# One core, four layers: lag of two tiles in the bit stage, bf16 openings of three recurrent stages, unread products at an RNN's end

## The reference

```python
# _L0_cond2_ref and _L3_cond2_ref: an LSTM over 256 steps for 8 rows of 128
a = xw_t + prev_h @ Wh
i, f, o = sigmoid of three quarters of a;  g = tanh(the last quarter)
next_c = f * prev_c + i * g;  next_h = o * tanh(next_c)
# layer 2: the same LSTM (_L2_cond_ref); then a gated delta rule over its output
S = tanh(beta * S + (v - S @ kn) x kn);  out = Sq * silu(Sq), Sq = S @ q
# then a plain RNN over x + y @ W_out:  h = tanh(h @ Wh + xW_t)
# then _L2_ffn_ref, the bit feed-forward (128 -> 512 -> 128, 2048 tokens)
wq = clip(round(w * scale), -1, 1) / scale
xq = clip(round(x * 127 / max|x|), -128, 127) * max|x| / 127      # per token
return bitlinear(silu(bitlinear(x, w_gate)) * bitlinear(x, w_up), w_down)
```

## Time and profile before

| what | value |
|---|---|
| three runs | 2833.24, 2842.12, 2864.39 us (median 2842.12) |
| the profiled execution | 2834.13 us, of which the span from first to last instruction is 2832.3 us |
| granted TensorE clock, mean | 0.839 of full speed |
| busy share | PE 85%, PEld 60%, DVE 58%, ACT 39%, POOL 27% |
| PEclk in 40 slices | 9997555555589999899999999999659955999998 |

### The profile page before, as it was taken

One profiled execution on the slowest core, in us unless ns is written; L12 is line 12 of the kernel. 1 busy time (PEld: TensorE's weight loads), 2 busy tenths in 40 slices (PEclk: granted clock), 3 DMA queues, 4 the chain that ended last, 5 costly groups with the idle time before them and its releaser, 6 DMA issues. The chain is left out here.

```text
span 2832.3 us, 91584 instructions
## 1 busy us (share of the span) xinstructions
PE 2407.7 (85%) x36874; PEld 1708.9 (60%) x36874; DVE 1648.4 (58%) x7006; ACT 1103.0 (39%) x4214; POOL 751.4 (27%) x1223
## 2 busy tenths in 40 slices
PE   5998878786399899779999999999658878999998
PEld 3555666665255456556666767665425556777774
DVE  3543555555545354357777777775345855667674
ACT  1332333332123343235555656564354423333332
POOL 1210000000122000127676767676243300000000
PEclk9997555555589999899999999999659955999998
DMA  2000000000100000125454545354100000000000
GB/s 97 3 3 2 2 2 2 3 2 2 40 2 3 2 1 0 70 54 116 104 116 101 118 100 121 96 121 109 45 1 1 2 2 2 2 3 3 2 3 15
DMA packets 110107, 104.24 MB, mean 37 GB/s; under 512 B 90496, under 2 KB 90496, under 8 KB 108800
## 3 DMA queue, kind: packets, MB, share of 16 engines
q1 hardware_dynamic: 109696, 98.50, 14.0%
HBM read 90.08 MB, written 8.39 MB: 35 GB/s over the span
## 5 line engine op out<-in xcount | busy, mean ns | idle before, releaser
L671 POOL TENSOR_TENSOR l2r_beta_s<-l2r_state,l2r_beta_f 128x256 f32<-128x256 f32 x512 | 370.0, 744 | 195.8 <-ACT l2r_state L574 194.6
L827 DVE TENSOR_TENSOR l2r_pre<-l2r_o_ps,l2r_beta_s 128x256 f32<-128x256 f32 x512 | 197.4, 419 | 85.7 <-PE l2r_o_ps L454 77.2
L574 ACT ACTIVATE l2r_state<-l2r_pre 128x256 f32<-128x256 f32 x512 | 190.0, 417 | 50.8 <-DVE l2r_pre L827 50.0
L140 PE MATMUL l0r_bank<-main_x,l0r_wx_half 128*128 128x32 f32 (+2 forms) x480 | 147.2, 406 | 60.7 <-ACT l0r_out_gate L196 60.1
L140 PEld LDWEIGHTS l0r_bank<-main_x,l0r_wx_half 128*128 128x128 f32 x480 | 116.0, 303 | 81.9 <-ACT l0r_out_gate L196 79.7
L1824 PEld LDWEIGHTS l3r_bank<-main_x,l3r_wx_half 128*128 128x128 f32 x480 | 95.6, 225 | 90.0 <-issue 44.8
L442 PE MATMUL l2r_d_ps<-l2r_state,l2r_kq 128*32 128x128 f32 x2056 | 148.0, 280 | 0.9 <-ACT l2r_state L574 0.7
L194 ACT ACTIVATE l0r_gates<-l0r_bank 128x24 f32<-128x24 f32 x256 | 48.6, 190 | 234.3 <-PE l0r_bank L152 234.3
L1963 ACT ACTIVATE l3r_gates<-l3r_bank 128x24 f32<-128x24 f32 x256 | 48.6, 190 | 222.8 <-PE l3r_bank L1836 222.8
L454 PE MATMUL l2r_o_ps<-l2r_rows,l2r_outer 32*128 32x128 f32 x2048 | 129.8, 323 | 4.6 <-DVE l2r_rows L819 1.3
L1807 POOL TENSOR_SCALAR main_y<-l3r_h_ring 128x128 f32<-128x128 f32 x16 | 8.4, 528 | 472.0 <-DVE l3r_h_ring L2117 472.0
(11 more groups left out here) (591 smaller groups left out, 7015.6 us busy)
## 6 DMA issues: line engine op xcount, KB each, us to landing
l2r_beta_f<-l2r_beta_store SPq DMA_DIRECT2D x256, 256.0 KB, 3.3
main_odd_layers<-in_l SPq DMA_DIRECT2D x1, 4826.5 KB, 14.6
main_odd_layers<-in_l SPq DMA_DIRECT2D x1, 3928.0 KB, 16.9
l2r_v_store<-l2r_v_part SPq DMA_DIRECT2D x32, 96.0 KB, 5.8
l2r_v_rows<-l2r_v_store SPq DMA_DIRECT2D x16, 192.0 KB, 4.6
main_decay<-in_decay SPq DMA_DIRECT2D x1, 3072.0 KB, 10.0
main_even_layers<-in_l SPq DMA_DIRECT2D x1, 2762.5 KB, 9.2
l2r_beta_store<-l2r_beta_tok SPq DMA_DIRECT2D x128, 16.0 KB, 1.6
```

The lines of the kernel that those rows point to most:

```text
L140: nc.tensor.matmul(into, wx_half[:, g * P:(g + 1) * P], x_b[:, :, w * LW + lo:w * LW + hi].rearrange("p b t -> p t b"), start=False, stop= ...
L574: nc.scalar.activation(state[:, h * 2 * P:(h + 1) * 2 * P], pre[:, h * 2 * P:(h + 1) * 2 * P], ACT.Tanh).then_inc(state_ready[h], 1)
L671: nc.gpsimd.tensor_tensor(beta_s[:, half].rearrange("p (g r) -> p g r", g=HG), state[:, half].rearrange("p (g r) -> p g r", g=HG), beta_f[ ...
L827: nc.vector.tensor_tensor(pre[:, half].rearrange("p (c n) -> p c n", c=2), o_ps[:, 2 * h:2 * h + 2, 0:P], beta_s[:, half].rearrange("p (c ...
```

## The change

It makes seven edits in four stages.

1. In l0r and l3r the two opening products read the high halves of `wx` and `x` as bf16 and no longer wait for `wx_half`; ACT makes `w_scaled` in POOL's place; only pieces 0, 4, 8 and 12 stand ahead of step 0, and the other eleven follow behind steps 2 to 10 (`FIRST_PIECES`), each behind a wait for that step's output gate.
2. In l2r step 0 waits for `wide_ready`, behind the third of POOL's clears, in place of `consts_ready` behind the last. The clear of `v_rows` goes from POOL to DVE as 2048 words; it, the clear of `state` and the copies into `r_ring` and `selv_bf` stand behind the split of h0.
3. `SQ_STEPS` moves two sums of the output from steps 4 and 7 to 5 and 8.
4. In the bodies in which neither LSTM nor delta rule runs, two unread products stand behind each step; body 20 has such steps too.
5. In l2f ACT applies a silu to `magic`, which nobody reads, ahead of the first `scale_input`.
6. In l2f PE, ACT and DVE handle tile n-2 where they handled n-1: `turn_prod(n-1)` is last in PE's turn, `copy_prod(n-2)`, `gate(n+1)` and `scale_output(n-2)` stand ahead of `scale_prod(n)`, and `product(n)` ahead of `add_output(n-2)`.
7. In l2f the next group's input is measured, scaled and rounded behind tile 4g, not 4g+1, and its integers are turned behind 4g+2, not 4g+3.

```diff
+FIRST_PIECES = {2: (1, 5), 3: (9,), 4: (13, 2), 5: (6,), 6: (10,), 7: (3,), 8: (7,), 9: (14,), 10: (11,)}
 # lstm_stage, lstm_expert_stage: gpsimd
-                nc.gpsimd.tensor_scalar(w_scaled[:, 0:3 * P], wh[:, 0:3 * P], 0.25, None, ALU.mult).then_inc(s["w_split"], 1)
 # tensor
+                for k in range(2):
+                    last = nc.tensor.matmul(bank[k][:, :], high(wx[:, 0:P]), high(x[:, 0:CHUNK]), start=True, stop=True, skip_group_check=True)
+                last.then_inc(s["opened"], 1)
                 pe.wait_ge(s["wx_ready"], 2)
-                for piece in range(LW - 1):
+                for piece in (0, 4, 8, 12):
                     inputs(0, piece)
                 pe.wait_ge(s["w_split"], 6)
                 for n in range(T):
                     step_products(n)
                     w, m = divmod(n, LW)
+                    for piece in FIRST_PIECES.get(n, ()):
+                        pe.wait_ge(s["o_ready"], n + 1)
+                        inputs(0, piece)
 # scalar
+                nc.scalar.activation(w_scaled[:, 0:3 * P], wh[:, 0:3 * P], ACT.Identity, scale=0.25).then_inc(s["w_split"], 1)
+                nc.scalar.activation(w_scaled[:, 3 * P:4 * P], wh[:, 3 * P:4 * P], ACT.Identity, scale=0.5).then_inc(s["w_split"], 1)
 # recurrent_stages
-SQ_STEPS = (0, 1, 2, 3, 4, 6, 7, 9)
+SQ_STEPS = (0, 1, 2, 3, 5, 6, 8, 9)
-UNREAD = {(True, False): 2, (True, True): 1, (False, True): 4, (False, False): 0}
+UNREAD = {(True, False): 2, (True, True): 1, (False, True): 4, (False, False): 2}
-                pe.wait_ge(s["consts_ready"], 2)
+                pe.wait_ge(s["consts_ready"], 1)
                 lstm_bias(0, 0)
                 for g in range(4):
                     lstm_inputs(0, 0, g)
                 pe.wait_ge(s["w_split"], 4)
+                pe.wait_ge(s["wide_ready"], 1)
 # bit_ffn_stage: gpsimd; the same shift for measure_input on DVE and scale_input on ACT
-                    if n % GROUP == 1 and n // GROUP + 1 < NG:
+                    if n % GROUP == 0 and n // GROUP + 1 < NG:
                         round_input(n // GROUP + 1)
 # vector
                 for n in range(NT + 2):
+                    if n < NT:
+                        product(n)
...
                     if n >= 2:
                         add_output(n - 2)
```

More of the change, by code:

```diff
@@ L906, in _ @@
                                         ALU.subtract).then_inc(s["bias_split"], 1)
-                nc.vector.tensor_copy(selv_bf[:, :], sel_v).then_inc(s["consts_ready"], 1)
                 split_alone(-1)
+                nc.vector.tensor_copy(r_ring[:, SLOTS - 1, :], h0).then_inc(s["r_ready"], 1)
+                nc.vector.memset(v_rows[:, :, :, :], 0.0).then_inc(s["rows_clear"], 1)
+                for h in range(2):
+                    nc.vector.memset(state[:, h * 2 * P:(h + 1) * 2 * P], 0.0).then_inc(state_ready[h], 1)
+                nc.vector.tensor_copy(selv_bf[:, :], sel_v).then_inc(s["selv_ready"], 1)
                 for k in range(BODIES + 1):
@@ L1911, in experts @@
                         last.then_inc(s["turn_psum"], 1)
+                for k in range(2):
+                    last = nc.tensor.matmul(bank[k][:, :], high(wx[:, 0:P]), high(x[:, 0:CHUNK]), start=True, stop=True, skip_group_check=True)
+                last.then_inc(s["opened"], 1)
                 pe.wait_ge(s["wx_ready"], 2)
-                for k in range(2):
-                    last = nc.tensor.matmul(bank[k][:, :], wx_half[:, 0:P], x[:, 0:CHUNK], start=True, stop=True, skip_group_check=True)
-                last.then_inc(s["opened"], 1)
-                for piece in range(LW - 1):
+                for piece in (0, 4, 8, 12):
                     inputs(0, piece)
@@ L2549, in _ @@
                 gate_and_up(0)
-                for n in range(NT + 1):
-                    if n >= 1:
-                        turn_prod(n - 1)
-                    if n % GROUP == 3 and n + 1 < NT:
-                        turn_integers(n // GROUP + 1)
+                for n in range(NT + 2):
                     if n + 1 < NT:
                         gate_and_up(n + 1)
-                    if n >= 1:
-                        down(n - 1)
                     if n % GROUP == 0 and n // GROUP + 1 < NG:
                         turn_input(n // GROUP + 1)
-                    if n >= 1:
-                        turn_output(n - 1)
+                    if n >= 2:
+                        down(n - 2)
+                        turn_output(n - 2)
+                    if n % GROUP == 2 and n // GROUP + 1 < NG:
+                        turn_integers(n // GROUP + 1)
+                    if 1 <= n <= NT:
+                        turn_prod(n - 1)
             @block.scalar
@@ L2606, in _ @@
                 act.wait_ge(s["magic_ready"], 1)
+                nc.scalar.activation(table_in[:, :], magic[:, :], ACT.Silu)
                 for n in range(GROUP):
```

55 lines of the change are left out of this document (26 added, 29 removed).

## The result

Four runs of the changed kernel took 2799.47 to 2813.95 us, median **2807.26**; four of the kernel before 2833.24 to 2864.39, median 2841.68. The ratio is 0.9875, 95% interval 0.9831 to 0.9920. It is faster by 1.3%, within the predicted range and 7 us above the predicted time. The profiled execution took 2809.66 us (span 2807.9), 24.5 less than the profiled one before.

The account below looks back on a forecast made before the run. The kernel was taken as a row of stages whose times add, the bit stage waiting on a loop through all engines. Gains of 18.1 + 0.6 + 2 x 3.0 + 6.0 + 5 + 0.2 = 35.9 gave 2800 us, range 2782 to 2826.

Parts of the forecast that it names:

- The ring through the addition: Bit stage before: a loop through all engines, where the next product waits for the last tile's addition, 4.48 us a tile.
- PE's queue with two trips to ACT: Bit stage after: PE's in-order work, including waits for ACT, was to be the longest, at 2.6 us a tile.
- the sum: Whole kernel: all terms of the forecast added up, 35.9 us less; as it stands given a chance of 0.55.
- 3 x 3.3: Bit stage: the group's measuring (about 2.4 us) and turning of integers (0.9) were to lengthen PE's loop once a group.
- 24 less: Bit stage: upper bound of the gain in us, if all four engines stay at 2.7 and the group's work is hidden.
- rival (d): Bit stage: POOL's rounding stretched from 1.92 us by DVE; at 5.6 the whole would reach 2842; chance 0.03.
- PE adds four pieces at 3.91/15 = 0.26: Openings of l0r and l3r: each input piece ahead of step 0 was to cost PE 0.26 us.
- Of which PE's idle time of 0.17 a step hides 9 x 0.17 = 1.5: l0r and l3r: eleven late pieces cost 2.9 us, idle time hides 1.5, so 1.3 is given back.
- The 1.4: Openings of l0r and l3r: gain in us per stage if POOL's work holds the bias copies up to 2 us.
- a sign of being wrong: Openings of l0r and l3r: the prediction would be wrong if step 0 waits for the bias.
- if the clock then stays at 2.4 GHz, 27 steps save 0.2: RNN's end: unread products hold the clock, saving 4.8 us; body 20's 32 products cost 5.2, of which 0.6 is covered.
- Rival (c): RNN's end: unread products do not hold the clock, or body 20's run at 1.2 GHz: +8 us, 2808; chance 0.1.

Follow-up runs that it names:

- run 1: The kernel before with only the changed bit stage (l2f): median 2811.75 us, ratio 0.9910 to before.
- run 7: The changed kernel with the bit stage's old tile order (lag of one) and three unread products per step in l2r's first body: 2814.04 us, executed once.
- run 9: The changed kernel without unread products at the RNN's end, with three in l2r's first body and the wide bias first in l0r and l3r: 2798.19 us, ratio 0.9852.
- run 3: The changed kernel with the sums of the output back in steps 4 and 7: median 2804.65 us, ratio 0.9869 to before.
- runs 4, 5 and 7: The changed kernel with: 15 (l0r) and 8 (l3r) pieces ahead, 2798.88 us; fp32 (l0r) and extra (l3r) opening products, 2799.47; run 7, 2814.04.

## Why the prediction was right, point by point

**The bit stage** (18.1 predicted, 21.6 measured, 20.4 alone in run 1). The mechanism was right: run 1 shows the gain in this stage alone and run 7 that edit 6 carries it. The ring through the addition before, and PE's queue with two trips to ACT as the next bound at 2.66 a tile (2.61 in the sum), are read from the timelines. The term was too small by the group's work: I had 3 x 3.3 for it, and 45.6 less 15 x 2.66 leaves 5.7 (with the last tiles at a granted 1.00), or 6 to 7 in the other kernels. The scalings and the rounded input overlap PE's loop more than I let them. The bound of "24 less" does not follow from its own condition, since 15 x 2.7 leaves 26.7; nor does rival (d)'s price, as 20 roundings at 5.6 in place of 3.6 are 40 us and not 36. Rival (d) did not come: all 16 roundings of the product took 1.92. **The early silu**: outside the loop the stage took 20.77 before and 20.25 after, 0.5 (0.6 predicted).

**The openings of l0r and l3r** (3.0 each predicted, 1.0 measured in l0r: 455.0 and 455.1 with the old opening, 453.8 to 454.3 with the new). Two terms were mis-sized. "PE adds four pieces at 3.91/15 = 0.26": they took 0.45 each, since the row that I priced them from stood at a granted 1.00 and the openings with bf16 products all stand at 0.50. "Of which PE's idle time of 0.17 a step hides 9 x 0.17 = 1.5": the eleven late pieces cost 2.8, not 1.3. And the bias copy was held: the case that the page "SBUF — State Buffer" of the Trainium skill ("Who interferes with whom") spoke for, by which a DVE copy in a two-port mode, or a DVE instruction with two SBUF inputs beside a POOL one that reads SBUF, and POOL's exclude each other for a whole instruction. 1.18 beside 1.15, and 1.05 beside 1.15 in run 9, agree with it. The 1.4 that the text gave for it was nearer than my 3.0, though run 9 prices the hold alone at 0.3 in l0r and 0.6 in l3r; the pieces were the larger part. POOL's chain ended 1.2 earlier against the stage's start, as forecast (though 1.84 less 0.8 is 1.0). But step 0 did not wait for it: POOL's last part was done at 249.84, and the weights of step 0 load at 250.24, behind the pieces that waited for the bias. I had named that as a sign of being wrong. In l3r, from the stage's start to the h of step 15, 0.9 was won (1.1 in l0r), and the later waves lost 4.6, for a reason that stays open.

**The opening of l2r** (6.0 predicted): 6.2 to the first h, less 0.4 to 2.0 in wave 0. The clear took 1.76 (2.2 estimated). The clock's fall in wave 0 was not in the sum.

**SQ_STEPS** (5 predicted): 5.8 by run 3, with the split that I gave, step 7 to 8 alone. The 2.8 us of wave 13 come on top, by the clock.

**The RNN's end** (0.2 gained predicted): in the changed kernel's trace this step failed. I wrote "if the clock then stays at 2.4 GHz, 27 steps save 0.2", and the clock fell behind 12 of 32 steps. Rival (c) came in its place: the tail behind the last step is 6.5 us longer, where (c) had 8. In runs 4, 5 and 7 the condition was met, and the terms were near: the steps saved 6.8 (4.8 in the sum) and body 20's products cost 4.7 (5.2 less 0.6), 2 us gained. So I treated as one value what is one of two, 2 gained or 6 lost, and gave (c) a chance of 0.1 where it came in four of seven traces.

**The whole.** That the time came out 7 us from the forecast is partly luck. The sum had 35.9; the spans of the two traces differ by 24.4, that is 11.5 less. Against the terms the bit stage gave 3.4 more; l2r gave 5.3 less, l0r 2.3 less, l3r 6.7 less and the rest of the program 0.6 less, and without the 2.8 of wave 13 l2r would stand at 8.1 less. The medians differ by 34.4, near the sum, only because before's median lies 7.6 above its profiled execution and the changed kernel's 2.4 below its own.

**Left open**: the place of the clock's steps in l3r, with the stage at 547.4 to 556.1 us, a spread larger than what any opening here won; and whether the clock holds to the RNN's end.
